# A two-lane decoder kernel: pads zeroed amid the experts, the rotation's root taken last, tanh routing, cross attention's reciprocal products on GpSimd, and a new order table

## What is computed

```python
x = LN(x + mamba(x))          # selective scan: 256 channels, 16 states, 512 steps
x = LN(x + cross16x64(x, c))  # own layernorm first; softmax over 32 keys, tanh(gate)
x = LN(x + experts(x))        # shared + 8 experts of 512, gelu; top 2 by softmax
x = LN(x + window(x))         # 16 heads of 8, rotary, 128 keys back
x = LN(x + cross16x8(x, c))
x = LN(x + local(x))          # 2 inner layers: shift, l2norm(q), l2norm(k), rotary with
                              # scales, 64 keys back, then layernorm and a gated MLP of 341
```

## Time and profile before

| | us |
|---|---|
| three runs: 1661.01, 1656.44, 1656.91; median | 1656.91 |
| the profiled execution, its own time | 1651.61 |
| its span in the trace | 1649.8 |
| TensorE busy (share of the span) | 1377.5 (83%) |
| VectorE busy | 1080.7 (66%) |
| ScalarE busy | 835.1 (51%) |
| GpSimd busy | 326.7 (20%) |

### The profile page before, as it was taken

The page is one execution under the profiler, slowest core; times in us unless marked ns, Lnnn a source line. Parts: engine busy times, 40 slices in busy tenths (PEclk is TensorE's granted clock), DMA queues, the critical chain, the costliest instruction groups (busy, mean ns, idle before and its releaser), DMA issues. The chain is left out here.

```text
span 1649.8 us, 23108 instructions
## 1 busy us (share of the span) xinstructions
PE 1377.5 (83%) x8604; PEld 862.6 (52%) x8604; DVE 1080.7 (66%) x2223; ACT 835.1 (51%) x2060; POOL 326.7 (20%) x212
## 2 busy tenths in 40 slices
PE   6877679998899788888875777899989987878885
PEld 3522236676666446546631223567756654654662
DVE  5789975115787777467447998711378878745853
ACT  3265426432765256665647552353357635665652
POOL 0136520002000042032001664100110004302400
PEclk9779978999999889998977888999999998999997
DMA  5500000000000010000000000000000000100000
GB/s 206 211 32 1 0 1 26 1 0 1 1 1 2 10 36 20 1 20 14 8 13 13 0 1 0 14 14 1 0 1 2 2 1 14 27 1 14 20 8 13
DMA packets 12928, 30.90 MB, mean 19 GB/s; under 512 B 1425, under 2 KB 5905, under 8 KB 12562
## 3 DMA queue, kind: packets, MB, share of 16 engines
q1 hardware_dynamic: 8978, 23.14, 3.8%
q10 hardware_dynamic: 3840, 6.29, 1.7%
HBM read 17.89 MB, written 5.24 MB: 14 GB/s over the span
## 5 line engine op out<-in xcount | busy, mean ns | idle before, releaser
L840 POOL TENSOR_TENSOR scratch<-scratch 128x1024 f32<-128x1024 f32 x64 | 150.0, 2353 | 197.3 <-DVE scratch L807 175.1
L659 PE MATMUL psum<-scratch,w_const 128*128 128x512 f32 x256 | 152.8, 730 | 23.3 <-POOL scratch L840 23.3
L1015 ACT ACTIVATE scratch<-psum,w_experts 128x512 f32<-128x512 f32 x144 | 98.2, 687 | 136.5 <-PE psum L971 133.3
L565 POOL TENSOR_SCALAR rstd<-mv 128x4 f32<-128x4 f32 x28 | 7.2, 258 | 786.6 <-DVE mv L552 786.6
L807 DVE TENSOR_TENSOR_SCAN scratch<-psum,scratch 128x512 f32<-128x512 f32 x128 | 151.3, 1210 | 13.9 <-ACT psum L732 13.3
L995 PEld LDWEIGHTS psum<-expert_weights,scratch 128*128 128x128 f32 x1152 | 134.7, 192 | 19.4 <-issue 18.9
L971 PE MATMUL psum<-xT,expert_weights 128*128 128x512 f32 x288 | 136.2, 606 | 1.0 <-ACT scratch L1015 1.0
L995 PE MATMUL psum<-expert_weights,scratch 128*128 128x128 f32 x1152 | 136.1, 275 | 0.6 <-DVE y L1060 0.5
L1060 DVE SCALAR_TENSOR_TENSOR y<-psum,comb,y 128x128 f32<-128x128 f32 x128 | 36.0, 344 | 146.0 <-PE psum L995 146.0
L1499 ACT ACTIVATE scratch<-psum,mx 128x128 f32<-128x128 f32 x256 | 90.1, 374 | 73.1 <-DVE mx L1590 73.0
L732 ACT ACTIVATE psum<-scratch,a_neg 128x512 f32<-128x512 f32 x128 | 87.9, 690 | 77.1 <-DVE scratch L807 60.0
(11 more groups left out here) (229 smaller groups left out, 3067.9 us busy)
## 6 DMA issues: line engine op xcount, KB each, us to landing
scratch<-scratch ACTq DMA_DIRECT2D x48, 128.0 KB, 2.3
expert_weights<-in_expert_weights SPq DMA_DIRECT2D x9, 512.0 KB, 9.5
folded_products<-expert_weights SPq DMA_DIRECT2D x8, 512.0 KB, 3.6
folded<-folded_products SPq DMA_DIRECT2D x8, 512.0 KB, 3.4
w_local<-in_local SPq DMA_DIRECT2D x1, 3122.0 KB
scratch<-in_cross SPq DMA_DIRECT2D x1, 2624.5 KB, 12.8
x<-in_x SPq DMA_DIRECT2D x4, 256.0 KB, 3.1
out<-xT SPq DMA_DIRECT2D x4, 256.0 KB, 2.4
```

What stands on the lines that cost most here:

```text
L659: ins = pe.matmul(sum_banks[c], ident, t.m.hC[:, 2 * ((n - 1) % 2) + c, :], start=(n == 1), stop=(n == NS))
L840: t.eng.tensor_tensor(t.m.hC[:, 2 * (n % 2):2 * (n % 2) + 2, :], t.m.hs[:, n % 2], C, ALU.mult)\
L1015: act.activation(t.m.hid[:, k % 2, f, :], t.a.take(), ACT.Gelu_apprx_tanh, bias=W("experts", "b1")[:, c:c + 1]).then_inc(t.s["a_freed"], 1)
```

## The change

- **Pads.** `hid` and `combT` move 10·T columns up in the scratch buffer, clear of the pads. In `experts_pool` the three memsets come first, waiting for `comb_ready`, and the norm's root behind them.
- **Roots.** The addition of eps and the maximum with 1e-24 move from GpSimd to VectorE (in mamba eps stays on GpSimd); GpSimd keeps the power. `norm_vector` and `squares` get one step more.
- **Rotation.** `rotate` multiplies unnormalised values by the tables (two products with the sine table instead of four, one with the cosine table instead of two), adds, and multiplies by the root last.
- **Routing.** th = tanh(g/2) on ScalarE; weights 0.5 − 0.5·th and 0.5 + 0.5·th in two VectorE instructions instead of three.
- **Cross attention.** The product with the reciprocal (L927) moves to `cross_pool`, behind a new semaphore `rinv_ready`; VectorE's reciprocal is no longer waited for by VectorE itself.
- **Order table.** All four engines' turns are new. The shown lines are the first of each; the rest is left out.

```diff
--- before.py
+++ after.py
 TURNS = {
     "pe": [
-        5, 18, 4, 8, 1, 8, 5, 3, 3, 2, 3, 4, 3, 1, 6, 2, 3, 3, 3, 3, 2, 1, 1, 2, 3, 3, 2, 1, 1, 2, 3, 3, 3, 3,
...
+        5, 31, 3, 2, 1, 1, 1, 5, 3, 4, 2, 1, 6, 2, 3, 3, 3, 3, 3, 3, 3, 3, 3, 3, 3, 3, 3, 3, 3, 3, 3, 3, 3, 3,
...
     "act": [
-        3, 1, 3, 1, 11, 1, 4, 1, 2, 3, 2, 2, 1, 1, 1, 3, 2, 2, 5, 1, 2, 2, 1, 2, 1, 1, 2, 1, 1, 2, 2, 1, 1, 2,
...
+        3, 1, 2, 1, 9, 2, 1, 3, 2, 2, 3, 1, 1, 5, 4, 1, 1, 1, 2, 1, 1, 2, 1, 1, 2, 2, 1, 1, 2, 2, 1, 1, 2, 2, 1,
...
     "dve": [
-        6, 2, 1, 8, 1, 8, 4, 1, 1, 1, 1, 1, 1, 1, 1, 1, 1, 2, 1, 2, 1, 3, 1, 5, 4, 1, 2, 3, 2, 2, 3, 1, 1, 4, 2,
...
+        6, 22, 1, 1, 1, 8, 3, 1, 1, 1, 1, 2, 4, 1, 3, 5, 4, 5, 1, 1, 1, 3, 2, 1, 1, 1, 2, 1, 1, 2, 2, 1, 1, 2,
...
     "pool": [
-        4, 2, 6, 1, 1, 1, 1, 1, 1, 1, 1, 1, 1, 1, 1, 1, 1, 1, 1, 1, 1, 4, 2, 1, 2, 6, 2, 2, 2, 2, 2, 2, 2, 2, 2,
...
+        3, 2, 4, 1, 1, 1, 1, 1, 1, 1, 1, 1, 1, 1, 1, 1, 1, 1, 1, 1, 1, 1, 1, 1, 1, 1, 1, 4, 2, 1, 1, 1, 3, 2, 1,
...
 }
@@ -362,7 +369,7 @@
             again(i)
             m.e1, m.pT1 = carve(i, 2, T), carve(i, 2, 4, P)
 
-            again(i)
+            again(i, 10 * T)
             m.hid, m.combT = carve(i, 2, NF, T), carve(i, T)
 
             again(i)
@@ -550,7 +557,8 @@
             yield from t.w.step(ins)
             for i in range(NT):
                 ins = t.eng.bn_aggr(t.m.mv[:, i, :], t.m.rowstat[:, i, :])
-            ins.then_inc(t.s["stats_ready"], 1)
+            yield from t.w.step(ins)
+            t.eng.tensor_scalar(t.m.rstd[:, :], t.m.mv[:, :, 1], EPS, None, ALU.add).then_inc(t.s["stats_ready"], 1)
             yield
             t.w(t.s["rstd_ready"])
             for i in range(NT):
@@ -560,16 +568,14 @@
             yield
             t.w(t.s[done])
 
-        def inverse_root(t, dst, src, op, by, done):
-
-            yield from t.w.step(t.eng.tensor_scalar(dst, src, by, None, op))
-            t.eng.tensor_tensor(dst, dst, W("const", "neg_half").to_broadcast([P, dst.shape[1]]), ALU.pow)\
-                .then_inc(t.s[done], 1)
+        def inverse_root(t, v, done):
+
+            t.eng.tensor_tensor(v, v, W("const", "neg_half").to_broadcast([P, v.shape[1]]), ALU.pow).then_inc(t.s[done], 1)
 
         def norm_pool(t):
             yield
             t.w(t.s["stats_ready"])
-            yield from inverse_root(t, t.m.rstd[:, :], t.m.mv[:, :, 1], ALU.add, EPS, "rstd_ready")
+            inverse_root(t, t.m.rstd[:, :], "rstd_ready")
 
 
         def turn_tensor(t, src):
@@ -825,7 +831,8 @@
             if t.row == 0:
                 t.eng.wait_ge(t.s["start_loaded"], 16 * len(FIRST))
             t.w(t.s["squares_ready"])
-            yield from inverse_root(t, t.m.rstd[:, :], t.m.small[:, 0, 0:NT], ALU.add, EPS, "rstd_ready")
+            yield from t.w.step(t.eng.tensor_scalar(t.m.rstd[:, :], t.m.small[:, 0, 0:NT], EPS, None, ALU.add))
+            inverse_root(t, t.m.rstd[:, :], "rstd_ready")
             t.skip(v=NB + 1)
             if t.row:
                 t.w.count(t.s["states_used"], 1)
@@ -922,9 +929,7 @@
                     yield
                     t.w(t.s["e_ready"])
                     yield from t.w.step(dve.tensor_reduce(t.m.sums[:, j, 0:H1], heads(t.m.e1[:, j, :]), X, ALU.add))
-                    yield from t.w.step(dve.reciprocal(t.m.rinv[:, j, 0:H1], t.m.sums[:, j, 0:H1]))
-                    e = heads(t.m.e1[:, j, :])
-                    dve.tensor_tensor(e, e, wide(t.m.rinv[:, j, 0:H1]), ALU.mult).then_inc(t.s["prob_ready"], 1)
+                    dve.reciprocal(t.m.rinv[:, j, 0:H1], t.m.sums[:, j, 0:H1]).then_inc(t.s["rinv_ready"], 1)
                     t.skip(a=1)
                 if i < NT:
                     if i >= 1:
@@ -942,6 +947,12 @@
         def cross_pool(t, inner):
             if inner:
                 yield from norm_pool(t)
+            for i in range(NT):
+                yield
+                t.w(t.s["rinv_ready"])
+                e = t.m.e1[:, i % 2, :].rearrange("p (h k) -> p h k", h=H1)
+                by = t.m.rinv[:, i % 2, 0:H1].rearrange("p (h o) -> p h o", o=1).to_broadcast([P, H1, S])
+                t.eng.tensor_tensor(e, e, by, ALU.mult).then_inc(t.s["prob_ready"], 1)
             yield from norm_pool(t)
             t.skip(a=1 + NT, v=NT, o=1)
 
@@ -1004,7 +1015,7 @@
             t.skip(v=1)
             yield
             t.w(t.s["gap_ready"])
-            act.activation(t.m.small[:, 1, 0:NT], t.m.small[:, 0, 0:NT], ACT.Exp).then_inc(t.s["ratio_ready"], 1)
+            act.activation(t.m.small[:, 1, 0:NT], t.m.small[:, 0, 0:NT], ACT.Tanh, scale=0.5).then_inc(t.s["ratio_ready"], 1)
             for k in range(E + 1):
                 yield
                 for f in range(NF):
@@ -1038,9 +1049,8 @@
             dve.tensor_copy(top, t.m.i8[:, :, 0:2])
             yield
             t.w(t.s["ratio_ready"])
-            yield from t.w.step(dve.tensor_scalar(t.m.small[:, 3, 0:NT], t.m.small[:, 1, 0:NT], 1.0, None, ALU.add))
-            yield from t.w.step(dve.reciprocal(t.m.small[:, 4, 0:NT], t.m.small[:, 3, 0:NT]))
-            yield from t.w.step(dve.tensor_tensor(t.m.small[:, 5, 0:NT], t.m.small[:, 4, 0:NT], t.m.small[:, 1, 0:NT], ALU.mult))
+            dve.tensor_scalar(t.m.small[:, 4, 0:NT], t.m.small[:, 1, 0:NT], -0.5, 0.5, ALU.mult, ALU.add)
+            yield from t.w.step(dve.tensor_scalar(t.m.small[:, 5, 0:NT], t.m.small[:, 1, 0:NT], 0.5, 0.5, ALU.mult, ALU.add))
             wide = lambda v: v.rearrange("p (t o) -> p t o", o=1).to_broadcast([P, NT, E])
             iota = W("const", "iota").rearrange("p (o e) -> p o e", o=1).to_broadcast([P, NT, E])
             for n, dst in ((0, t.m.comb[:, :, 0:E]), (1, t.m.eqt[:, :, :])):
@@ -1067,10 +1077,12 @@
 
         def experts_pool(t):
             t.skip(v=1 + E + 1, a=2 + (E + 1) * NF)
-            yield from norm_pool(t)
+            yield
+            t.w(t.s["comb_ready"])
             t.eng.memset(t.m.vpad, 0.0)
             t.eng.memset(t.m.qpad, 0.0)
             t.eng.memset(t.m.kpad, 0.0).then_inc(t.s["pads_ready"], 1)
+            yield from norm_pool(t)
 
 
 
@@ -1541,32 +1553,29 @@
                 if i >= 1:
                     yield
                 dve.wait_ge(t.s["a_freed"], t.a.at)
-                dve.tensor_reduce(t.m.small[:, 2 * (i % 2), 0:16], t.m.sqs.rearrange("p (h d) -> p h d", h=2 * H5), X,
-                                  ALU.add).then_inc(t.s["ss_ready"], 1)
+                ss = t.m.small[:, 2 * (i % 2), 0:16]
+                yield from t.w.step(dve.tensor_reduce(ss, t.m.sqs.rearrange("p (h d) -> p h d", h=2 * H5), X, ALU.add))
+                dve.tensor_scalar(t.m.small[:, 2 * (i % 2) + 1, 0:16], ss, 1e-24, None, ALU.max)\
+                    .then_inc(t.s["ss_ready"], 1)
 
             def rotate(i, turned):
-                h = lambda v: v.rearrange("p (h d) -> p h d", h=2 * H5)
-                yield
-                t.w(t.s["root_ready"])
-                rn = t.m.small[:, 2 * (i % 2) + 1, 0:16].rearrange("p (h o) -> p h o", o=1).to_broadcast([P, 2 * H5, DH5])
-                yield from t.w.step(dve.tensor_tensor(h(t.m.qk[:, i % 2]), h(t.m.qk[:, i % 2]), rn, ALU.mult))
+                yield
                 if i >= 1:
                     dve.wait_ge(t.s["a_freed"], turned)
-                for q in range(2):
-                    own = slice(q * 512, (q + 1) * 512)
-                    halves = lambda v: v[:, own].rearrange("p (h a d) -> p h a d", h=H5, a=2)
-                    for a in range(2):
-                        by = tab5[:, l, 2 * q + 1, i:i + 1, 32 * a:32 * a + 32].to_broadcast([P, H5, 32])
-                        ins = dve.tensor_tensor(halves(t.m.turned)[:, :, a, :], halves(t.m.qk[:, i % 2])[:, :, 1 - a, :],
-                                                by, ALU.mult)
+                halves = lambda v: v.rearrange("p (q h a d) -> p q h a d", q=2, h=H5, a=2)
+                table = lambda k, z: tab5[:, l, k:4:2, i:i + 1, z].to_broadcast([P, 2, H5, z.stop - z.start])
+                for a in range(2):
+                    ins = dve.tensor_tensor(halves(t.m.turned)[:, :, :, a, :], halves(t.m.qk[:, i % 2])[:, :, :, 1 - a, :],
+                                            table(1, slice(32 * a, 32 * a + 32)), ALU.mult)
                 yield from t.w.step(ins)
-                for q in range(2):
-                    own = slice(q * 512, (q + 1) * 512)
-                    z = lambda v: v[:, own].rearrange("p (h d) -> p h d", h=H5)
-                    ins = dve.tensor_tensor(z(t.m.qk[:, i % 2]), z(t.m.qk[:, i % 2]),
-                                            tab5[:, l, 2 * q, i:i + 1, :].to_broadcast([P, H5, DH5]), ALU.mult)
+                z = t.m.qk[:, i % 2].rearrange("p (q h d) -> p q h d", q=2, h=H5)
+                ins = dve.tensor_tensor(z, z, table(0, slice(0, DH5)), ALU.mult)
                 yield from t.w.step(ins)
```

(9 more changed lines are left out.)

2 lines of the change are left out of this document (1 added, 1 removed), and 97 rows, old and new, of the table TURNS.

## The result

The changed kernel takes 1601.1 us (median of 4 runs, 1595.33 to 1603.6), the kernel before 1658.13 us in the runs beside it: ratio 0.9649, 95% interval 0.9619 to 0.968. The profiled execution took 1595.33 us, its span is 1593.5 us. Over all series the kernel before took 1638.69 to 1673.25 us, 2% from end to end and not 0.3%: a difference of 5 us between two kernels here is not told from 0.

A forecast was written before the change was run, and what follows sets the result against it. It saw TensorE bound in the experts, VectorE in the state loop, neither full in local layers and joints. Terms −8 − 8 − 8 + 7 = −17 us gave 1634.6 us in the trace, near 1640 measured; range 1616 to 1662.

The forecast's parts named there:

- order table: All engines' turns: TensorE's nearly unchanged from windowed attention to local; three places differ, priced +7, 0 and 0 us.
- Pads, -8: Row ends of the experts: earlier memsets end the stall of VectorE's normalising products; -8 us, bounds 0 and -9.5.
- Rotation, -8: Local layer starts: table products run under GpSimd's power, TensorE comes late next; 4 × 2 = -8 us, bounds -19.7 and 0.
- Cross attention, -8: 32 products leave VectorE for GpSimd, TensorE binds next: -5 us for second cross attention, -3 for first; bounds -22 and +11.
- Norm and routing, 0: Eps additions moved to VectorE cost nothing; routing's two fewer VectorE instructions are hidden by TensorE's full experts stretch: 0 us.
- Start, +7: Setup products in one block delay lane 0's first scan from 62 to 74 us: +7 us, bounds 0 and +18.
- Lead, 0: Lane 0 leads by about 2 states instead of 5, rows enter cross attention almost together: 0, within 5 us either way.
- second head, 0: Before the second pair of rows both tails run in step: 0, within 5 us either way.
- more than forecast: Rival: the evener order closes further idles between stages, -30 to -45 us, about 1620 us; chance 0.13.
- port lock: Rival: each rotation is held by shared SBUF ports until its own row's power ends, 1694 us; chance 0.03.

The follow-up runs named there:

- x11: All changed steps, new rotation (root product last) included, in the order table of the kernel before, same table as x9: 1645.69 us, ratio 0.9959 to the kernel before.
- x10: Changed kernel with the order of the kernel before up to the first experts and the new order from there: 1619.58 us, ratio 0.9742 to the kernel before.
- x4: Changed kernel with the pads' memsets put back behind the row's norm on GpSimd: 1608.83 us, ratio 0.9703 to the kernel before.
- x14: x11 with the reciprocal products of cross attention back on VectorE: 1645.4 us, ratio 0.9926 to the kernel before.
- x15: x11 with the pads' memsets back behind the norm on GpSimd: 1660.12 us, ratio 0.9994 to the kernel before.
- x7: Kernel before with 31 of lane 1's 34 setup products in one block, on TensorE and VectorE: 1658.29 us, ratio 0.9995 to the kernel before.
- x12: Steps of the kernel before, with the new order up to the first experts and the old order from there: 1660.13 us, ratio 1.0044 to the kernel before.
- x9: Changed steps in the order of the kernel before, but with the old rotation, root product first: 1646.15 us, ratio 0.9893 to the kernel before.
- x6: Changed kernel with the rotation's root product back in front of the table products: 1640.07 us, ratio 0.9893 to the kernel before.
- x5: Changed kernel with the 32 reciprocal products of cross attention back on VectorE: 1618.01 us, ratio 0.9771 to the kernel before.
- x1: Changed kernel with lane 1's setup products again spread between lane 0's first steps: 1621.58 us, ratio 0.9752 to the kernel before.
- x8: Changed kernel with the old order from the last layer's closing steps on: 1612.8 us, ratio 0.972 to the kernel before.
- x2: All changed steps with the order table of the kernel before carried over step by step: 1659.43 us, ratio 0.999 to the kernel before.

## Why the prediction was wrong

The direction was right, and so were three mechanisms; the sum was 40 us short. The step that failed is the **order table**: "From windowed attention to local, TensorE's sequence is nearly the old one. Three places differ." I priced the edits by the waits of the old order and the table by itself, as a sum of places. The two don't add: all edits in the old order came to 7 us by x11's ratio (13 by the medians), the new order around the old steps to a loss of up to 20, both together to a gain of 57. Most of it arises from the experts on (x10 against x11: 36 us), where I had put the order at nothing.

- **Pads, -8: right in the forecast's sense.** L565 takes 1.12 us at the row ends, in x4 4.15 again, and the price is -1 to 9 by the ratios, 3 to 8 by the medians. TensorE's waits for it fell from 14.7 to 3.6 us and are 8.9 in x4, and the expert stages give 4 us in the new order and 7 in the old; in the change they gained 13, the rest of which is the order's.
- **Rotation, -8: right for its mechanism, wrong for its size.** "What comes late next is TensorE" did not hold. In the old order it is ScalarE's squares, the sum of which VectorE makes next: 10.3 of the 16.5 us came back as a wait for them, and of the rest the times show nothing. (The two local stretches together took 461, 466 and 477 us in x14, x15 and x11, with the root last, and 470 to 478 in before, x7, x12 and x9, with the root first; a few us may be there.) In the new order the two lanes begin the local layers 7, 5, 7 and 1 us apart (7, 21, 6 and 8 before), so that both stand at the same wait and, as I read it, neither has work to put under the other's. What the trace shows is that the second lane waits longer at a layer's start: 3.0 to 5.7 us in x6, at most 1.4 in x9. The 30.1 us of waits in x6 cost 31 to 40. My bound of -19.7, the old order's whole wait, was no bound for the new one. Against the kernel before, the local stretches gained 12 us.
- **Cross attention, -8: too small by the times, about right by the traces.** The four stages gained 15 us in the first profile and 8 in the second; x5's undoing cost 11 to 20 by the ratios and 5 to 11 in these stages. I took 2.5 us a place because TensorE's 16.34 of 21 us would bind next and each unit's chain grew. So VectorE's time does count there in the new order, well inside the bound of 22; in the old order no worth of the same 22 us is seen (x14). The lanes' distance explains it at best in part: they enter the four stages 28, 8, 19 and 8 us apart in the old order and 14, 8, 16 and 8 in the new. The rest is open.
- **Norm and routing, 0.** Not tried by themselves. VectorE's wait for the root at L565, 12.3 us here and 14.1 before, speaks for nothing of note, and so do the expert stages of x15, which has these edits and takes 265 us there like the kernel before.
- **Start, +7: the wrong sign.** The estimate took the setup products at the durations of the trace of before, 3.10 to 3.68 us for sixteen. Those were taken at a granted clock near half. In one block they took 2.00 us, the last of the setup began at 50.50 instead of 63.81, and lane 1's transposes came at 62 us instead of 77, where I had let its squares begin 2.5 us sooner. x1 prices this order at 7 to 17 us. But x7 and x12 show no gain of it with the old order behind it.
- **Lead, 0, and second head, 0.** x10 against x1 shows no price of the lost lead, as forecast. The joint to the second pair is 2 us longer, the second state loop 6 shorter; inside the ends given, and not tried apart.
- **Closing steps.** Not in the prediction. In the trace the last 46 us became 39, and x8 gives 5 of them back.

Of the rivals, "more than forecast" came true, and beyond its 30 to 45 us. The port lock did not. By the Trainium skill's page "SBUF — State Buffer", section "Who interferes with whom", a product with two SBUF inputs contends with a GpSimd instruction that reads SBUF, over a shared port pair that it calls an exclusive lock. The traces here differ: the products beside a power take 1.30 and 1.23 us, of which the second has a mean of 1.22 over the whole run, and only the power grows, from 2.92 to 3.27.

What stays open: which places of the new order from the experts on make the edits pay, and why. I showed the effect by pairs, and its place only as far as x10 and x11 do; and single profiles of one order differ by up to 11 us in a local stretch (242 us in x11, 231 in x15), so differences below that in one profile of these stages prove little.

## What to carry to other kernels

Where the order of two interleaved rows is written out by hand, an edit is not worth the wait that it removes in the old trace. Its worth depends on whether the other row covers that wait, and a new order changes the cover: price edits and order together, and when you test them apart, use pairs with the same table. Where the times of two kernels lie within their noise, a stage that repeats from profile to profile can still tell them apart, as the experts and the closing steps did here. And read the granted clock beside any duration that you carry into a sum.

## What was unexpected of the hardware

The same order of the setup products met two clocks. With the products mixed into lane 0's first steps, TensorE was busy 14.00 of 14 us from 38 to 52 us in every profile, and the granted clock there was 0.50 or 0.51 (1.2 GHz) in five (before, x1, x9, x14, x15) and 1.00 (2.4 GHz) in three (x2, x10, x11). With the block it was 1.00 in all nine. First x1, then x10, each from 38 to 52 us:

```profile
38.00:52.00 14.00, 14.00 (x84) 12.78 (x81) 7.86 (x10) 4.14 (x4) 0.00 (x0) 0.50 0.22 87
```

```profile
38.00:52.00 14.00, 14.00 (x121) 11.34 (x121) 13.78 (x19) 3.85 (x4) 0.00 (x0) 1.00 0.52 208
```

In the same 14 us x1 did 84 matmuls and x10 121. From 26 to 38 us, before this stretch, TensorE worked 10.85 of 12 us in the kernel before and 11.83 in the changed one. What tips it is open: x2 also had 10.85 there, and the full clock. Each kernel has one profile, so how often the mixed order meets the low clock isn't known either.
